# Post-norm attention and gated MLP: another order of tiles in the phase of scores

## The reference

```python
qkv = x @ Wqkv                                   # 16 heads of 16
logits = einsum('bihd,bjhd->bhij', q, k) * 0.25 + slope[h] * (j - i)
logits = where(i >= j, logits, -inf)             # causal
attn = softmax(logits) ; a = einsum('bhij,bjhd->bihd', attn, v) @ Wout
x1 = layernorm(x + a)
gate, up = x1 @ wg.T, x1 @ wu.T                  # 768 wide, int weights / 127
out = layernorm(x1 + (silu(gate) * up) @ wd.T)
```

## Time and profile before

| | |
|---|---|
| Median of 3 runs | 2172.32 us (2170.78 to 2173.74) |
| The profiled execution | 2172.58 us, span in the trace 2170.9 us |
| TensorE (PE) busy | 2004.1 us, 92% |
| VectorE (DVE) busy | 1598.7 us, 74% |
| ScalarE (ACT) busy | 1231.3 us, 57% |
| GpSimd (POOL) busy | 927.6 us, 43% |
| Mean granted TensorE clock | 0.981 |

### The profile page before, as it was taken

How to read it: one execution, slowest core, us unless ns; L and a number is a source line. 1 busy time by engine, 2 the same in 40 slices (tenths; PEclk the granted TensorE clock), 3 DMA queues, 4 the chain that set the end, 5 groups by cost and what they waited for, 6 DMA issues and landing times.

```text
span 2170.9 us, 47760 instructions
## 1 busy us (share of the span) xinstructions
PE 2004.1 (92%) x19236; PEld 1543.8 (71%) x19236; DVE 1598.7 (74%) x2765; ACT 1231.3 (57%) x1999; POOL 927.6 (43%) x1924
## 2 busy tenths in 40 slices
PE   4789999999999999999999999999999999999986
PEld 3557777777767767767767777777776776776766
DVE  4567777787777778777778777778777777877744
ACT  1445655555665655665556565555566565566542
POOL 0223444453444444444444344445344444444444
PEclk8799999999999999999999999999999999999998
DMA  7455545445545545545545554554564553554400
GB/s 201 101 118 104 121 106 104 108 100 104 128 100 109 117 94 107 117 112 105 114 96 110 105 122 105 104 108 100 105 127 100 108 118 92 109 116 103 85 16 20
DMA packets 148830, 229.09 MB, mean 106 GB/s; under 512 B 13552, under 2 KB 64496, under 8 KB 148592
## 3 DMA queue, kind: packets, MB, share of 16 engines
q1 hardware_dynamic: 148608, 226.02, 47.5%
HBM read 139.98 MB, written 84.93 MB: 104 GB/s over the span
## 4 chain that ended last, share of the span: by engine, by line
PE 71%; POOL 13%; ACT 6%; DVE 5%; issue 2%; DMA 2%; SPq 1%; POOLq 0%; DVEq 0%
PE pair L486 63%; PE pair L489 8%; ACT probs L717 5%; POOL probs L894 4%; POOL x L914 3%; POOL rstd L911 2%; POOL result L927 2%; DVE stats L865 1%; DVE result L861 1%; POOL rstd L924 1%; DVE staged_lo L777 1%; ACT staged_hi L695 1%; DMA q_rows<-max_lo 1%; POOL mean L909 1%; POOL var L908 1%
## 5 line engine op out<-in xcount | busy, mean ns | idle before, releaser
L717 ACT ACTIVATE probs<-pair 128x1024 f32<-128x1024 f32 x640 | 633.8, 1025 | 244.0 <-PE pair L486 243.7
L901 POOL TENSOR_TENSOR h_lo<-h_full,h_hi 128x256 fp32r<-128x256 f32 x384 | 283.3, 738 | 604.3 <-ACT h_hi L742 593.6
L894 POOL TENSOR_SCALAR_AFFINE_SELECT probs<-probs 128x256 f32<-128x256 f32 (+1 forms) x896 | 369.0, 442 | 385.1 <-ACT probs L717 380.8
L486 PE MATMUL pair<-q_rows,k_rows 64*128 64x512 f32 (+3 forms) x2048 | 324.1, 374 | 88.6 <-DVE staged_lo L777 38.9
L792 DVE TENSOR_REDUCE row_max<-pair 128x2 f32<-128x1024 f32 x256 | 312.1, 1219 | 80.5 <-PE pair L486 80.5
L486 PEld LDWEIGHTS pair<-q_rows,k_rows 64*128 64x128 f32 x2048 | 165.3, 188 | 281.8 <-ACT probs L717 162.4
L794 DVE TENSOR_REDUCE row_max<-pair 128x8 f32<-128x1024 f32 x256 | 312.7, 1221 | 59.5 <-PE pair L486 59.3
L486 PE MATMUL pair<-probs,v_ones 128*32 128x512 f32 (+3 forms) x4096 | 334.1, 444 | 23.1 <-POOL probs L894 22.7
L486 PE MATMUL pair<-k_rows,q_rows 52*128 52x512 f32 (+3 forms) x2048 | 295.2, 350 | 5.4 <-DMA q_rows<-bounce 2.3
L695 ACT ACTIVATE staged_hi<-pair 128x512 fp32r<-128x512 f32 x128 | 76.7, 599 | 286.7 <-PE pair L486 277.5
L734 ACT ACTIVATE h_full<-pair 128x256 f32<-128x256 f32 x384 | 145.1, 378 | 125.5 <-PE pair L486 124.6
(11 more groups left out here) (88 smaller groups left out, 3725.5 us busy)
## 6 DMA issues: line engine op xcount, KB each, us to landing
bounce<-staged_hi SPq DMA_DIRECT2D x128, 256.0 KB
bounce<-staged_lo SPq DMA_DIRECT2D x128, 256.0 KB
q_rows<-bounce SPq DMA_DIRECT2D x128, 256.0 KB, 5.0
k_rows<-bounce SPq DMA_DIRECT2D x128, 256.0 KB, 6.3
x_sb<-L_attn_x SPq DMA_DIRECT2D x32, 512.0 KB, 9.1
k_rows<-bounce SPq DMA_DIRECT2D x128, 128.0 KB, 5.4
q_rows<-bounce SPq DMA_DIRECT2D x128, 128.0 KB, 6.5
x<-L_attn_x SPq DMA_DIRECT2D x32, 512.0 KB, 8.8
```

The source lines that it names most:

```text
L486: return tensor.matmul(o, lhs, rhs, start=start, stop=stop, skip_group_check=True, **kw)
L717: scalar.activation(probs[g][:, tile, :, :], pair[:, :, :], ACT.Exp, scale=scale).then_inc(s_exp, 1)
L894: made = pool.affine_select(out=diagonal, in_=diagonal, compare_op=ALU.is_ge, fill=0.0, base=0, pattern=[[0, diagonal.shape[1]], [1, P]], ...
L901: pool.tensor_tensor(h_lo[:, m, :], h_full[(n_split_h[step] - 1) % H_BUFFERS][:, :], h_hi[:, m, :].bitcast(F32), ALU.subtract).then_inc(s_ ...
```

## The change

The table gets another order in its second half, the two parts of the first group's weighted sum stand next to each other, the two sets of pairs change places, and the second part of `norm1` is kept back until the select of tile 4.

```diff
 ATTENTION = ((S, 0), (F, 0), (S, 1), (F, 1), (S, 2), (F, 2), (V, -2, 1, 0), (S, 3), (F, 3), (F, 4), (S, 4), (V, -2, 1, 1),
-             (S, 5), (F, 5), (S, 6), (F, 6), (S, 7), (F, 7), (V, -1, 0, 0), (S, 8), (F, 8), (F, 9), (S, 9), (V, -1, 0, 1))
+             (F, 5), (S, 5), (F, 6), (S, 6), (F, 7), (V, -1, 0, 0), (V, -1, 0, 1), (S, 7), (F, 8), (S, 8), (F, 9), (S, 9))
+NORM_BEHIND = 4
...
-        self.order = []
+        self.order, self.norms_due = [], []
...
+    def norms(self):
+        for step in self.norms_due:
+            self.add(*step)
+        self.norms_due = []
...
         pairs = self.by_age(range(BANKS // 2))
-        score_pairs, first_pairs = [pairs[1], pairs[3]], [pairs[0], pairs[2]]
+        score_pairs, first_pairs = [pairs[0], pairs[2]], [pairs[1], pairs[3]]
...
                 self.add("select", w - 1, k)
+                if k == NORM_BEHIND:
+                    self.norms()
...
+        self.norms()
         if self.has(w):
             self.add("combine", w)
...
                 self.add("norm1", done, 0)
-                self.add("norm1", done, 2)
+                self.norms_due.append(("norm1", done, 2))
             self.project(w + 2, 1)
```

## The result

The changed kernel takes 2136.98 us (median of 4 runs, 2136.29 to 2138.28) against 2172.15 us: a ratio of 0.9839, 95% interval 0.9821 to 0.9856, 35.2 us less. The forecast was 2140, with 2129 to 2156 as its range. The profiled execution took 2136.29 us, its span is 2134.6 us, 36.3 less than before.

A forecast was written before the change was run, and what follows sets the result against it. TensorE was taken to bound the rests, with idle time to win only in phases, and VectorE as second limit. 21.8 + 9.3 + 4.8 - 3.4 = 32.5 us gained, giving 2140 us; own range 2132 to 2149, 8 in 10 within 2129 to 2156.

The forecast's parts named there:

- The norm's second part: Norm phases: kept back, it lets selects finish before the sum; phase falls to plain length, 29 x 0.75 = 21.8 us.
- The second half of the table: Phase's second half: new order brings F7 to 9.39, phase 14.56 instead of 14.72 us; 9.3 us gained in 58 phases.
- The pairs: Phase's first half: S1 starts earlier, but F2 still waits for F0's row maximum; counted at 0.
- The rests: Between phases: VectorE's late row maximum and combine fit ahead of their readers; cost 0, bound up to 0.3 us a rest.
- First units: Run's start: gather goes out 1.14 us later, delaying S0 in three early units; 3.4 us lost, bounds 0 and 6.
- rival D: Steady even rests: later gather pushes row maxima's DMA past S0; slower, 2198 us if 3.6 beyond the figures; chance 4%.
- Last unit: Run's end: selects finish earlier, so sum and x1t_hi come earlier; 4.8 us less, bounds 2.5 and 5.5.
- parts 2 and 4: The phase's second half (9.3 us gained) and the run's ends (4.8 gained, 3.4 lost); their bounds gave the range.
- part 2: Phase's second half under the new order: 0.16 us less a phase, bounds 0 and 0.4.
- A: Phase's first half gains as well because F2 is not held: 21 us more, 2119 us; chance 4%.
- B: VectorE becomes the bound; its backlog eats the second half's gain and costs 0.3 us each odd rest: 2158 us; chance 10%.
- C: Weighted sum still waits for GpSimd, selects being late by the exponentials, not the norm: 2162 us; chance 3%.

The follow-up runs named there:

- e1_norm_only: Kernel before with one edit, the second part of norm1 kept back behind the select of tile 4; old table order and pairs: 2147.11 us.
- e3_pairs_only: Kernel before with only the two sets of pairs exchanged between score tiles and first-pass tiles: 2172.36 us.
- e4_all_but_pairs: Changed kernel with the old line for the pairs, keeping the new order and the norm's move: 2141.67 us.
- e5_all_but_norm: Changed kernel with the second part of norm1 back where it was, keeping the new order and pairs: 2177.93 us.
- e2_order_only: Kernel before with only the new second half of the table, pairs and norm as before: 2176.52 us.
- e8_short_staged_lo: Changed kernel with staged_lo of the keys' projection made for 128 of 512 columns from unit 2 on, output not the reference's: 2114.15 us.
- e6_sum_ahead_of_s4: Changed kernel with the second part of the second group's weighted sum moved ahead of score tile S4: 2105.1 us.
- e7_sum_ahead_of_f2: As e6_sum_ahead_of_s4, with that sum's first part also ahead of F2 and its second part ahead of F4: 2127.3 us.

## Why the prediction was right

**The norm's second part** was put at 21.8 us and at nothing in cost. e1_norm_only gives 25.0 for it, where 21.8 and about 2.5 in the last unit were expected: 21.9 in the steady part, the rest behind it.

**The second half of the table** was put at 0.16 us a phase; it is 0.22. The chain that was named is the one that acts: F7 behind F5's row maximum, the undivided sum, F8's row maximum, the rest. Two of its sizes were off and nearly cancel. F5's row maximum starts 0.62 behind F5 in its new place, not 0.50, so F7 is at 9.51 and not 9.39. And the sum takes 2.29 us (1019.63 to 1021.92) where the two parts apart took 0.99 and 1.43: undivided it is 0.13 shorter, which I had not counted. F8's row maximum is then 0.04 closer to its F8. 58 x 0.22 + 29 x 0.75 is 34.5; the steady part gained 34.2. So the mechanism was right, and the closeness of the size (14.56 against 14.50) is in part luck: the errors have opposite signs.

**The pairs** were put at nothing. By themselves they are (e3_pairs_only). Beside the new order they are worth 0.07 us a phase or 4 us (e4_all_but_pairs), by a path that I had not seen, read from the trace: the exponential of S1 and the sum that takes its pair. With the old pairs the new order gives 0.16 a phase and not 0.22. F1 waits until 1.57 and not 1.48, and F2 is at 2.62 as foretold.

**The rests** did not grow, as foretold: VectorE's backlog of maxima at their start fitted ahead of the divide: in the odd rest attn is ready 1.90 us past the start (forecast at most 2.18), and its transposes start at 2.34.

**First units**: forecast 3.4 us lost, measured 2.3. The gather does go out later: at 109.34 where the earlier trace rows has 108.35, and S0 follows at 125.44 where it was 124.41, 16.10 behind it against 16.06. But nearly half of this is the phase itself, which starts at 93.66 and not 93.21: within it the gather goes out 0.54 us later, not the 1.14 that I took from the steady phases, where it holds (14.59 against 13.45). The three stretches from one S0 to the next that end in such a wait are 0.7, 0.6 and 0.8 us longer than before (27.77, 31.78 and 28.16 us against 27.09, 31.21 and 27.37), so the forecast's 3 x 1.14 was too large in its size per wait.

```profile
109.34 0.60 SPq L471 DMA_DIRECT2D q_rows<-bounce  x1
```

```profile
125.44 0.79 PE L495 MATMUL pair<-q_rows,k_rows 64*128 64x512 f32 x2 [6.73 <-DMA q_rows<-max_lo]
```

In the steady even rests the gather is 17.6 us ahead of S0 (forecast 17.67) and no S0 waits, so rival D had 1.5 us to spare there; only S0 of unit 62, behind a shorter rest, waits 0.51 us. The kernels with the new order all begin unit 4 later than the one before, but by anything from 0.6 us (185.75, e5_all_but_norm) to 4.9 (190.07, e4_all_but_pairs); e1_norm_only does not, and e3_pairs_only, with the old order, begins it at 186.56. How much of the 2.3 us is the gather, and how much the clock of these early units, stays open.

**Last unit**: from S0 to x1t_hi it was 2101.83 - 2081.08 = 20.75 us and is 2064.78 - 2048.95 = 15.83, 4.9 less for a forecast of 4.8. The first group's sum there ran at 2.4 GHz, where the earlier trace rows have the granted clock at 0.50:

```profile
2059.15:2061.44 2.29, 2.29 (x32) 0.94 (x32) 0.00 (x0) 0.86 (x1) 2.10 (x5) 1.00 0.00 0
```

The wait ahead of it was 0.41 us and the clock stayed up. But the forecast's "full clock" did not hold in this unit as a whole: just before, from S4 to S5, the granted clock was 0.52, where in the same place of the kernel before it was 1.00 (before, then after):

```profile
2086.24:2088.10 1.86, 1.86 (x28) 0.98 (x28) 0.00 (x0) 1.02 (x1) 1.69 (x3) 1.00 0.76 189
```

```profile
2054.09:2057.45 3.36, 3.35 (x28) 1.40 (x29) 0.00 (x0) 1.02 (x1) 3.25 (x8) 0.52 0.75 234
```

In this unit TensorE had waited 0.88, 0.41 and 1.12 us by then, always for exponentials; before, it had waited 0.35, 0.27, 0.41 and 1.12 there without a fall. The same 28 matmuls took 1.5 us more. By an estimate this cost the sum about 0.5 us: it started at 2059.15, behind the exponential of S5, while the selects were through at 2058.63 (2055.84 + 2.79). So 4.9 for 4.8 is in part luck: this loss was not foreseen, and the undivided sum's 2.29 us and an x1t_hi that does not wait for the last exponential's end made up for it. The rule of the Trainium skill that the prediction named ("TensorE: Matmul & The Clock Gate", "HAM oscillation"), that short idle stretches do not bring the throttled clock, agrees with the wait of 0.41 us. It does not agree with this fall, nor with those in e2_order_only and e5_all_but_norm, behind 0.36 and 0.83, and 0.35 and 0.93 us; there the measurement decides.

**The range.** The forecast's own range, 2132 to 2149, was said to be parts 2 and 4 between their bounds. By those bounds it is wider: part 2 alone, at 0.4 us a phase instead of 0.16, would give 14 us more, 2126. The measured 2137 lies inside either.

Of the rivals, A (the first half gains too) fell with e3_pairs_only and e8_short_staged_lo, B with the unchanged rests, C with e1_norm_only, D as said. The expectations of the experiments did worse than the prediction: they missed the clock in two, the coupling of pairs and order in a third, and the size of e6_sum_ahead_of_s4; in e7_sum_ahead_of_f2 the rival was right and the theory wrong.

## What to carry to other kernels

When two engines are nearly full, read the chain that passes through both: here a tile of the first pass, its maximum on VectorE, and the next tile that needs its banks. A wait on TensorE that this chain overtakes costs nothing (the 0.67 us ahead of S1), and filling idle time of TensorE so that the other engine starts later costs more than it gives (2127 against 2105 us). An edit that is worth 25 us alone may be what makes another one pay: the new order and pairs lost 6 us without the norm's move and gained 10 with it, so try the halves of a change together before one is dropped.

## What the runs showed of the hardware

- Waits of TensorE of 0.81 to 0.83 us (e2_order_only) and 0.93 to 0.95 us (e5_all_but_norm), with 0.36 or 0.35 just before, stand in all 58 norm phases of the two traces. In 9 of them the granted clock fell to 1.2 GHz behind the waits, which made the phase about 1.7 us longer. With 0.69 it was not seen in the 29 norm phases of the kernel before.
- In the last unit of the changed kernel the granted clock was 0.52 behind waits of 0.88, 0.41 and 1.12 us; behind 0.35, 0.27, 0.41 and 1.12 us in the same place of the kernel before it was 1.00. So the length of the single waits does not tell by itself whether the clock falls.
- A matmul step that has to wait on two semaphores, the first of them the late one, started 0.14 to 0.15 us behind the end of staged_lo, which it waited for; with one semaphore it was 0.05 (1.57 and 1.48 of the phase, changed kernel and kernel before).
- 32 matmuls of a weighted sum in one row take 2.29 us at the full granted clock, as 8 and 24 with other work between them 0.99 and 1.43.
